# LayerNorm fused into the output projection, weight loads cut in halves, and another cadence of side work in a four-sublayer transformer kernel on eight Trainium2 cores

## The reference, cut to what matters

```python
x = L0_attn_a_x                                   # [8, 2048, 1024] f32
x = x + attn_a(layernorm(x), ...)                 # causal attention, 16 heads of 64
x = x + ffn(layernorm(x), ...)                    # full attention, each projection with
                                                  # rank-16 experts, top 2 of 8, added
x = x + attn_b(layernorm(x), ...)                 # retention scan along the sequence,
                                                  # its own LayerNorm, silu gate
x = x + ffn(layernorm(x), ...)                    # the same ffn and weights again
def layernorm(x, eps=1e-5):
    m = mean(x); v = var(x); return (x - m) / sqrt(v + eps)
```

## Time and profile before

| | us |
|---|---|
| median of 2 runs | 4347.52 (4278.52 and 4416.52) |
| profiled execution | 4316.72 |
| its span, slowest core (core 4) | 4315.2 |
| spans of the 8 cores | 4256.3 to 4315.2 |
| busy: TensorE / ScalarE / VectorE | 3154.3 / 1492.0 / 1437.3 |

### The profile page before, as it was taken

How to read it: one execution, slowest core, us unless ns; L and a number is a source line. 1 busy time by engine, 2 the same in 40 slices (tenths; PEclk the granted TensorE clock), 3 DMA queues, 4 the chain that set the end, 5 groups by cost and what they waited for, 6 DMA issues and landing times. The chain is left out here.

```text
span 4315.2 us, 40631 instructions; the slowest of 8 cores (4256.3 to 4315.2 us)
## 1 busy us (share of the span) xinstructions
PE 3154.3 (73%) x13663; PEld 1295.6 (30%) x13815; DVE 1437.3 (33%) x2007; ACT 1492.0 (35%) x1488; POOL 65.3 (2%) x81
## 2 busy tenths in 40 slices
PE   3577777778446888888878456367277888888878
PEld 1223333225122333333335122122132333333344
DVE  5333333325552111111115546514632111111134
ACT  0035444450000666665660000120002656566640
POOL 0000000000000000000000000000000000000000
PEclk6788888879668888888889777678578888888889
DMA  2210000005221100000004310026111000000014
GB/s 89 27 12 6 5 6 6 1 1 144 110 39 20 10 5 6 6 6 1 1 3 130 122 24 16 0 58 215 29 20 15 6 6 6 5 6 1 1 40 137
DMA packets 91213, 144.39 MB, mean 33 GB/s; under 512 B 62057, under 2 KB 70394, under 8 KB 78604
## 3 DMA queue, kind: packets, MB, share of 16 engines
q1 hardware_dynamic: 18108, 104.04, 7.4%
q0 software_dynamic: 72912, 37.75, 6.6%
HBM read 145.97 MB, written 33.55 MB: 42 GB/s over the span
## 5 line engine op out<-in xcount | busy, mean ns | idle before, releaser
L735 ACT ACTIVATE ringf<-psd,negcb 128x1024 bf16<-128x1024 f32 x1024 | 1063.3, 1121 | 650.1 <-PE psd L683 649.4
L735 ACT ACTIVATE ringa<-psd,negcb 128x1024 bf16<-128x1024 f32 x320 | 340.5, 1120 | 373.8 <-PE psd L683 373.5
L663 PE MATMUL psb<-ringf,vprf 128*65 128x512 bf16 x1024 | 450.8, 440 | 16.9 <-ACT ringf L735 14.9
L680 PE MATMUL psd<-qpairf,kpairf 64*128 64x512 bf16 x1024 | 427.6, 430 | 24.7 <-ACT ringf L735 4.6
L683 PE MATMUL psd<-qpairf,kpairf 64*128 64x512 bf16 x1024 | 435.2, 437 | 0.0
L667 PE MATMUL psb<-ringf,vprf 128*65 128x512 bf16 x1024 | 429.5, 419 | 0.0
L637 PE MATMUL psb<-c_IDENT,densf 1*128 1x1 f32 x1024 | 181.1, 302 | 172.1 <-DVE act L837 172.1
L637 PEld LDWEIGHTS psb<-c_IDENT,densf 1*128 1x128 f32 x1024 | 177.5, 264 | 189.9 <-issue 189.9
L680 PEld LDWEIGHTS psd<-qpairf,kpairf 64*128 64x128 bf16 x1024 | 91.8, 95 | 459.0 <-issue 457.8
L663 PEld LDWEIGHTS psb<-ringf,vprf 128*65 128x65 bf16 x1024 | 114.7, 112 | 318.2 <-issue 312.3
L183 ACT ACT_TABLE_LOAD x4 | 5.1, 1283 | 575.6 <-DVE lnrcf L178 321.9
(11 more groups left out here) (250 smaller groups left out, 4173.0 us busy)
## 6 DMA issues: line engine op xcount, KB each, us to landing
lnstf<-Xs SPq DMA_DIRECT2D x16, 1024.0 KB, 5.5
xof<-Xs SPq DMA_DIRECT2D x16, 1024.0 KB, 7.4
lnsta<-xT SPq DMA_DIRECT2D x8, 1024.0 KB, 6.2
xoa<-xT SPq DMA_DIRECT2D x8, 1024.0 KB, 6.6
Xs<-xna SPq DMA_DIRECT2D x8, 1024.0 KB, 8.5
Xs<-xnf SPq DMA_DIRECT2D x8, 1024.0 KB, 8.9
lnstb<-Xs SPq DMA_DIRECT2D x8, 1024.0 KB, 5.1
xob<-Xs SPq DMA_DIRECT2D x8, 1024.0 KB, 6.5
```

The source lines that it names most:

```text
L663: t.matmul(PSB[4][0:65, :], VP[tkpv][:, hA * 65:hA * 65 + 65], RING[slot][:, 0:512], start=(tkpv == 0), stop=(tkpv == n - 1))
L680: t.matmul(pd[:, 0:512], KP[p % 2][0:64, ks], QP[p % 2][0:64, cs], start=True, stop=True, tile_position=(0, 0))
L735: ex.inc(s.activation(RING[slot][:], pd[:], AF.Exp, bias=NEGC[:, p:p + 1], scale=softmax_scale))
```

## The change

1. A class LN takes the place of `_ln_bodies`. In the three fused LayerNorms nothing is loaded again. ScalarE casts and squares XNEW as soon as the four residual additions of a tile are done, TensorE's column sums of tile dt2-2 stand ahead of the groups of tile dt2, and only the last two tiles' sums stand behind the last group. LayerNorm a1 keeps its loads; ScalarE does the squares there and VectorE the casts.
2. In all four the row arithmetic goes by chunks of 1x512, with the PSUM reads on ScalarE. Broadcast and normalization go chunk by chunk: eight multiplications, then eight subtractions, for each of four chunks.
3. Causal attention has `cad` 3 in place of 2. TensorE's g9 moves from slot 10 to 11 and g10 from 12 to 13, VectorE's last group from 13 to 14, in both kinds of attention.
4. Each 2 MB weight load of the output projections and the retention sublayer becomes two loads of 512 columns each, with a semaphore each; the second is waited for at dt2 = 4.
5. The output projection's block ends with a wait for its last stores.

```diff
+class LN:
+    CSB = (2, 3, 6, 7)
...
+    def cast_tile(self, s_, dt, src_ap):
+        nb = len(self.XSQ)
+        if dt >= nb:
+            s_.wait_ge(self.tc.sem, self.tc0 + dt - nb + 1)
+        if self.fused:
+            self.lns.inc(s_.activation(self.bufs["XLN"][dt][:], src_ap[:],
+                                       AF.Identity))
+        self.lns.inc(s_.activation(self.XSQ[dt % nb][:], src_ap[:],
+                                   AF.Square))
...
+    def vector_rows_norm(self, v):
+        P, bufs, XLN = self.P, self.bufs, self.bufs["XLN"]
+        for ch in range(NC):
+            cs = slice(ch * CH, (ch + 1) * CH)
+            v.wait_ge(self.sr.sem, self.srv[("m2", ch)])
+            P.vmark(v.tensor_mul(self.rowc[0:1, cs], self.rowa[0:1, cs],
+                                 self.rowa[0:1, cs]))
+            P.vjoin(v)
+            self.vr.inc(v.tensor_sub(self.rowc[0:1, cs], self.rowb[0:1, cs],
+                                     self.rowc[0:1, cs]))
+        for ch in range(NC):
+            cs = slice(ch * CH, (ch + 1) * CH)
+            v.wait_ge(self.sr.sem, self.srv[("ex", ch)])
+            self.vr.inc(v.tensor_mul(self.rowa[0:1, cs], self.rowa[0:1, cs],
+                                     self.rowb[0:1, cs]))
+            v.wait_ge(self.tb.sem, self.tb0 + ch + 1)
...
+    def tensor_bcasts(self, t, pre=None):
+        for ch in range(NC):
...
+            t.wait_ge(self.sr.sem, self.srv[("ex", ch)])
+            t.wait_ge(self.vr.sem, self.vrv[("murs", ch)])
+            t.matmul(bufs["PSB"][ch][:], bufs["ONESROW"][:],
+                     self.rowb[0:1, cs], start=True, stop=True)
+            self.tb.inc(t.matmul(bufs["PSB"][4 + ch][:], bufs["ONESROW"][:],
+                                 self.rowa[0:1, cs], start=True, stop=True))
...
-        cad = 2 if causal else 4
+        cad = 3 if causal else 4
...
             TS_MAP = {0: 0, 1: 1, 2: 2, 3: 3, 4: 4, 5: 5, 6: 6, 7: 7,
-                      8: 8, 10: 9, 12: 10}
+                      8: 8, 11: 9, 13: 10}
...
             VS_MAP = {0: 0, 1: 1, 2: 2, 3: 3, 4: 4, 5: 5, 6: 6, 7: 7,
-                      8: 8, 9: 9, 10: 10, 11: 11, 13: 12}
+                      8: 8, 9: 9, 10: 10, 11: 11, 14: 12}
...
-            g.dma_start(
-                WOB[:].rearrange("p (t o) -> p t o", t=ND),
-                bufs[wo_name][:].rearrange("(t p) o -> p t o", p=128)
-            ).then_inc(gq.sem, 16)
+            for j, ctr in enumerate((gq, gqb)):
+                ctr.inc(g.dma_start(
+                    WOB[:].rearrange("p (t o) -> p t o", t=ND)[
+                        :, :, j * 512:(j + 1) * 512],
+                    bufs[wo_name][:, j * 512:(j + 1) * 512].rearrange(
+                        "(t p) o -> p t o", p=128)), 16)
...
+                if dt2 == 4:
+                    t.wait_ge(gqb.sem, gqb0 + 16)
+                if ln is not None and dt2 >= 2:
+                    ln.colsums(t, dt2 - 2)
```

More of the change, by code:

```diff
@@ L221, in emit_ln, with _ @@
           nc.Block(f"ln_{tag}") as blk):
-        _ln_bodies(P, bufs, src, blk,
-                   ([xst0, xst1], [xsq0, xsq1], t1, rowa, rowb, rowc))
+        XST = [xst0, xst1]
+        ln = LN(P, bufs, ([xsq0, xsq1], t1, xst0, rowa, rowb, rowc),
+                fused=False)
+        lq = [P.c("lnq0"), P.c("lnq1")]
+        lq0 = [lq[0].v, lq[1].v]
+        @blk.sync
+        def _(sync):
+            for dt in range(ND):
+                if dt >= 2:
+                    sync.wait_ge(ln.lns.sem, ln.lns0 + dt - 1)
+                    sync.wait_ge(ln.vcp.sem, ln.vcp0 + dt - 1)
+                lq[dt % 2].inc(
+                    sync.dma_start(XST[dt % 2][:],
+                                   src[dt * 128:(dt + 1) * 128, :]), 16)
+        @blk.scalar
+        def _(s_):
+            for dt in range(ND):
+                s_.wait_ge(lq[dt % 2].sem, lq0[dt % 2] + 16 * (dt // 2 + 1))
+                ln.cast_tile(s_, dt, XST[dt % 2])
+            ln.scalar_rows(s_)
+        @blk.vector
+        def _(v):
+            for dt in range(ND):
+                v.wait_ge(lq[dt % 2].sem, lq0[dt % 2] + 16 * (dt // 2 + 1))
+                ln.copy_tile(v, dt, XST[dt % 2])
+            ln.vector_rows_norm(v)
+        @blk.tensor
+        def _(t):
+            for dt in range(ND):
+                ln.colsums(t, dt)
+            ln.tensor_bcasts(t)
 def emit_gate(P, bufs, tag):
@@ L1063, in _ @@
                     to.inc(last)
+            if ln is not None:
+                ln.colsums(t, ND - 2)
+                ln.colsums(t, ND - 1)
         @blk.vector
@@ L1085, in _ @@
                     vo.inc(ins)
[L1090 to L1098 removed]
+        if ln is not None:
+            @blk.scalar
+            def _(s_):
+                for dt in range(ND):
+                    s_.wait_ge(vo.sem, vo0 + nxvso_holder[0] + NC * (dt + 1))
+                    ln.cast_tile(s_, dt, XNEW[dt % 2])
+                ln.scalar_rows(s_)
+            @blk.vector
+            def _(v):
+                ln.vector_rows_norm(v)
+            @blk.tensor
+            def _(t):
+                ln.tensor_bcasts(
+                    t, pre=lambda t_: t_.wait_ge(
+                        vo.sem, vo0 + nxvso_holder[0] + NC * ND))
 def emit_attnb(P, bufs):
```

251 lines of the change are left out of this document (124 added, 127 removed).

## The result

The changed kernel's ratio to the kernel before is 0.9532, 95% interval 0.9515 to 0.9549, that is 4.7% faster. The medians of all executions are 4152.57 us (11 of it, 4072.27 to 4214.07) and 4285.25 us (10 of the kernel before). Its profiled execution took 4078.4 us, its slowest core (core 0) 4076.9 us, the other seven 4053.0 to 4075.7. In these comparisons the kernel before takes 4278 to 4286 us, so the starting point was 31 to 38 us too high, and the gain is some 200 us where I had worked out 183.

A forecast was written before the change was run, and what follows sets the result against it. LayerNorms ran one engine at a time, TensorE bound the projections, attention alternated Exp and TensorE. Fused LayerNorms net -92, a1 -8, weights -25, full attention -31, causal -27: -183 us from 4316.7, giving 4134 us, range 4050 to 4215.

The forecast's parts named there:

- three fused tails: LayerNorms f1, b1, f2 after the last residual addition: each falls to 76.3 us, shrinking by 123 us together.
- their sums in the projections: Output projections: 56 column-sum matmuls now stand in each, adding 10, 9 and 12 us, 31 in all.
- LayerNorm a1: First LayerNorm, which keeps its loads: casts -5, rows -7, normalization +4, together -8 us.
- weights in halves: Retention sublayer and its output projection: first halves land earlier, -6.1 us three times and -7 once, -25 us.
- full attention: The two ffns: the bound's wait goes, 2.2 us a pair for 7 pairs in each, -31 us.
- causal attention: Causal pairs: maxima's and bound's waits go, 3.9 us a pair net for 7 pairs, -27 us.
- the copy is covered: Causal pair's end: the copy into NEGC hides behind evictions TensorE awaits anyway; otherwise up to 2 us a pair return.
- 4.6 a pair: Causal attention: gain from two removed waits of some 2.3 us each, before 0.7 is given back.
- Table switching: Rival, LayerNorm rows on ScalarE: each change of function needs a table load, 36 us more, 4170 us; chance 0.07.
- Nothing is won in attention: Rival, both attentions: side work moves but waits only change names, 58 us of gain lost, 4192 us; chance 0.14.
- The casts keep up: Projections: 3.9 us of ScalarE work fits 8.6 us of groups; the late-casts rival loses 72 us, 4206 us, chance 0.05.
- The slower side: Rival, dense stages: the chip takes back density, clock 0.81, 216 us lost, 4350 us; limiter's chance 0.05.

The follow-up runs named there:

- e2_whole_weights: The changed kernel with each 2 MB weight load whole, as one DMA again; ratio 0.9558 to the kernel before, span 4095.4 us.
- e4_cad2: The changed kernel with `cad` 2 in causal attention, later slots kept; ratio 0.9522 to the kernel before, span 4075.0 us.
- e11_end2: Repeat of the changed kernel with mean products ahead of broadcasts, g8 at slot 9 and `cad` 2; two executions, 3985.6 and 3977.7 us.
- e12_end3: Repeat of the changed kernel with mean products ahead of broadcasts, g8 at slot 9, `cad` 3 kept; ratio 0.9323, span 3983.9 us.
- e8_cad2_g8: The changed kernel with mean products ahead of broadcasts, g8 at slot 9 and `cad` 2 in causal attention; ratio 0.9286, span 3972.2 us.
- e10_products_g8: The changed kernel with mean products ahead of broadcasts and g8 at slot 9, `cad` 3 kept; ratio 0.9274, span 3985.7 us.
- e1_attn_old: The changed kernel with attention's slot maps and `cad` as before the change; ratio 0.9655 to the kernel before, span 4131.7 us.
- e9_g8_slot9: The changed kernel with g8 moved from slot 8 to slot 9; two executions, 4044.3 and 4037.6 us.

## Why the prediction was right, and where its sizes were off

The sign, the range and the largest part of the mechanism held, but several sizes were off and partly cancelled. That the sum came within 10% of the measured gain is partly luck: the first, second and fifth rows below brought some 40 us more than forecast, the last some 12 us less, and the time was counted from an execution that lay 31 to 38 us too high, which is the larger part of the 56 us between 4134 and 4078.

| step | forecast, us | measured, us | from |
|---|---|---|---|
| three fused tails | -123 | -133 | windows: 352.2 before, 219.6 now |
| their sums in the projections | +31 | +8 | 62.6, 69.7, 69.5 against 58.7, 67.3, 67.5 |
| LayerNorm a1 | -8 | -7 | 41.0, 14.2, 53.5 against 44.4, 21.4, 50.2 |
| weights in halves | -25 | -23 | e2_whole_weights, in their stage |
| full attention | -31 | -38 to -40 | starts of Exp |
| causal attention | -27 | -14 to -16 | starts of Exp, all eight pairs |

**Tails.** The steps were cast and sums 7.7, rows 14.2, normalization 54.4. They measured 6.0, 14.3 and 53.4. The row chain with chunk 3's read in it was right to 0.1 us. The sums were faster than I took them, by the pairs of the next point. The 4 us of waiting at the head of each later chunk are there (4.07).

**The sums in the projections** is the step that failed most: "56 x 0.218 = 12.2 us". It priced each of the 56 matmuls as one that has TensorE to itself. They ran two at a time, so that a tile's eight took 0.97 us where I had 1.74. That makes seven tiles 6.8 us, and the 3 us of idle time that the projection had absorbed part of it: +3.9, +2.4 and +2.0 us. The third was also helped by the clock, 0.96 in its window where the earlier trace rows have 0.86; that isn't the change's doing. The eight cores' means (cores 0 to 3 for the kernel before) give +1.8, +5.5 and +2.5 us from first to last matmul, 10 us in all. The diff showed the sums of squares in row 32 beside those in row 0, and I did not ask what that row number was for.

**Weights.** In core 0 the first half landed 8.7 to 9.9 us after its issue in the retention sublayer and 13.7 us for the output projection, against 14.4, 14.6 and 17.9. I had taken 8.4, the landing of a load by itself. Over the eight cores the first matmul of a retention block came 8.3 to 11.1 us behind the issue, on five of them always within 9.0 us. So the step was right to 2 us.

**Attention, full.** "A pair gains 1.4 us at least, 3 us if slow steps become fast." The wait is gone in all seven pairs and nothing came in its place. The measured 2.4 to 3 us a pair lie at the upper end: the slow steps behind the wait went as well. ScalarE in the last chunk of a pair now (compare):

```profile
1751.63 0.20 ACT L778 ACTIVATE grow<-grow 1x1 f32<-1x1 f32 x1
1751.77 12.16 ACT L794 ACTIVATE ringf<-psd,negcb 128x1024 bf16<-128x1024 f32 x12
```

Behind the bound twelve Exps run at 1.01 us. In pairs 0 to 6 of the two ffns, 17 and 15 Exps stood 1.4 to 1.7 us behind the one before in the kernel before (core 4), and 1 and 2 do now (core 0); 7 more in each ffn stand 1.7 to 3 us behind, at other places.

**Attention, causal.** Both waits went as said, 35.7 us before against 3.3 now. Two steps of the sum failed, each by a part. One is "the copy is covered", with the 0.7 us a pair given back for the longer end. With three steps at a pair's end, the copy into NEGC was late on ScalarE's side: at the first Exp of the next pair it waited 4.4 us in six pairs, which isn't in the kernel before or in e4_cad2.

```profile
ACT ringa L794 <- DVE negcb L852: 26.4, 6, 4.4
```

VectorE's masks came later too, 36.1 us of waits in 53 against 17 to 18 in 36 to 40 with `cad` 2. The pairs with `cad` 2 put the longer end at 7 to 10 us over seven pairs, 1.0 to 1.4 a pair (e4_cad2 beside the change, e11_end2 beside e12_end3, e8_cad2_g8 beside e10_products_g8).

The other is that a wait taken away is time gained. e4_cad2 and e1_attn_old differ only in the slots, and with `cad` 2 in both the maxima's and the bound's waits go, 33 us of them (18.3 and 18.0 against 3.3), and the masks' waits stay. The seven pairs gained 21 us (644.4 to 623.7, means over the cores), not the 32 of "4.6 a pair". In core 0 of both, over the same seven pairs, TensorE was busy for 14 us more with the same matmuls (496.4 us in e1_attn_old, 510.7 in e4_cad2, 2043 records each), and the granted clock was 0.84 in e1_attn_old and 0.82 in e4_cad2. So 32 us of waits bought 21, the longer end took 10 back, and 11 are left. Which stretches lost the clock isn't shown. I also priced the squares' wait at 2.5 us by its row, where e9_g8_slot9 puts it at 3.6 with the slow steps behind it; but it cost that before the change as well.

**The rivals.** Table switching fell: one load a list, none between the rows. "Nothing is won in attention" fell for the ffns and came half true for the causal part. The casts keep up: TensorE was busy for 62.60 us of 62.60 in the first projection and 69.66 of 69.70 in the second; in the third, 66.38 of 69.50, it waited 3.0 us in four waits for VectorE's additions and not for a cast. The slower side wasn't seen in the changed kernel: the mean granted clock is 0.829 to 0.844 over the cores, not below that of the kernel before. But the trace that I started from has it: core 4 of the kernel before stood at a granted clock of 0.81 for 241 us in all, from 2834 us on (a window of 2945.8 to 2967.0, inside f2's projection, gives 0.81), and cores 5 to 7 for 221 to 245 us. Cores 0 to 3 never did, nor did any core in the changed kernel's trace. It has a part in the 0.86 of the earlier trace rows, and the cores that showed it took 4297 to 4315 us where cores 0 to 3 took 4256 to 4279. What brings it in wasn't tried.

## What to carry to other kernels

A wait on TensorE can cost its own length and the steps that follow at the half clock: here 2.56 us became 3.6, and moving the consumer by one slot brought 34 us in the whole kernel, 25 of them so explained. But waits taken away are not time gained one for one: 32 us of them bought 21 in causal attention. Price such a step by a run with that step alone. In a loop over chunks, small work of the next chunk that starts a hand-over to another engine belongs ahead of the long work of this one; left behind it, each turn cost 4.6 us of the longest engine, some 55 us in all. And where many matmuls have a narrow output, look to which row they write before pricing them one by one.

## What the hardware showed that was not expected

Single-row matmuls to rows 0 and 32 of one bank start 0.01 us apart and take the time of one, at either clock: pairs 0.21 us apart at a granted clock of 1.00 (above), and in a1 at 0.50 some 0.42 us:

```profile
47.52 0.63 PE L152 MATMUL psd<-xln,c_ONESB 128*1 128x512 bf16 x1
47.53 0.63 PE L157 MATMUL psd<-lnsqa,c_ONESB 128*1 128x512 bf16 x1
47.95 0.63 PE L152 MATMUL psb<-xln,c_ONESB 128*1 128x512 bf16 x1
```

A pair's length in causal attention is not smooth in what is taken from it. With the same instructions it was 86.2, 88.9 or 92.1 us in one core of e4_cad2. I read that as one slow stretch more or less, but only the stretch behind the squares' wait was followed row by row.
